# Rotary attention layer on one Trainium2 core: the depthwise convolution moved from the preparation to GpSimd in the attention loop, the values projected once and turned

## What is computed

```
q = xn @ wq.T + bq
k = (xn @ wk.T + bk) * scaling
v = xn @ wv.T + bv
lepe = conv_5x5(v, lepe_w, one filter per channel, padding 2) + lepe_b
qr, kr = theta_shift(q), theta_shift(k)        # x * cos + rotate_every_two(x) * sin, per head
attn = softmax(qr @ kr.T + mask)               # per image and head, 1024 x 1024
out = attn @ v + lepe
x = x + out @ wo.T + bo
```

## Time and profile before

| | us |
|---|---|
| median of three runs | 8046.31 |
| span of the profiled execution, first to last instruction | 8043.7 |
| what this span leaves to the median of the runs | 2.6 |
| layers 0 to 2, up to the rotary layer | 5577.0 |
| rotary preparation | 673.6 |
| rotary attention | 1793.1 |

### The profile page before, as it was taken

The page is one execution under the profiler, slowest core; times in us unless marked ns, Lnnn a source line. Parts: engine busy times, 40 slices in busy tenths (PEclk is TensorE's granted clock), DMA queues, the critical chain, the costliest instruction groups (busy, mean ns, idle before and its releaser), DMA issues. The chain is left out here.

```text
span 8043.7 us, 157230 instructions
## 1 busy us (share of the span) xinstructions
PE 7011.3 (87%) x56704; PEld 4290.7 (53%) x56704; DVE 4978.2 (62%) x7151; ACT 3803.5 (47%) x7049; POOL 2019.4 (25%) x2407
## 2 busy tenths in 40 slices
PE   3999999999877899469999999997776799999999
PEld 2555555555555556345555555553332466666665
DVE  4555555555555666445555555554888577777776
ACT  0444444444522555224444444443111577777777
POOL 3344344334220000043443443441111000000000
PEclk7999999999988989779999999998766899999999
DMA  7776776776459756477667667664222555455453
GB/s 160 154 140 122 139 136 117 138 140 122 88 178 216 133 110 122 103 163 141 124 129 142 126 124 140 133 123 96 77 72 72 138 124 136 121 130 130 120 135 88
DMA packets 500587, 1025.92 MB, mean 128 GB/s; under 512 B 80391, under 2 KB 276680, under 8 KB 460568
## 3 DMA queue, kind: packets, MB, share of 16 engines
q1 hardware_dynamic: 452694, 932.07, 53.5%
q0 software_dynamic: 47360, 86.53, 6.6%
HBM read 670.94 MB, written 358.93 MB: 128 GB/s over the span
## 5 line engine op out<-in xcount | busy, mean ns | idle before, releaser
L1512 DVE TENSOR_REDUCE a_nmp<-a_S 128x2 f32<-128x1024 f32 x1536 | 1878.8, 1224 | 1153.3 <-PE a_S L1357 1139.9
L1616 ACT ACTIVATE a_PROB<-a_T 128x512 f32<-128x512 f32 x3072 | 1667.7, 595 | 1750.0 <-PE a_T L1336 1742.5
L1215 POOL CAST a_RF<-a_RL 32x512 fp32r<-32x512 f32 x1536 | 1297.7, 845 | 1138.5 <-DVE a_RL L1540 1046.6
L2397 DVE CUSTOM_DVE_ANT_0 a_X<-a_S,a_mask 128x1024 f32<-128x1024 f32 x768 | 916.9, 1222 | 466.0 <-PE a_S L2293 462.3
L2440 ACT ACTIVATE a_PROB<-a_T 128x512 f32<-128x512 f32 x1536 | 836.3, 602 | 291.6 <-PE a_T L2307 291.6
L1332 PE MATMUL a_T<-a_QW,a_KW 64*128 64x512 f32 x3072 | 799.5, 513 | 181.1 <-ACT a_PROB L1616 108.2
L1332 PEld LDWEIGHTS a_T<-a_QW,a_KW 64*128 64x128 f32 x3072 | 309.5, 190 | 1161.0 <-issue 1157.9
L1370 PE MATMUL a_O<-a_PROB,a_V 128*32 128x512 f32 x6144 | 898.8, 660 | 2.5 <-ACT a_PROB L1616 2.5
L2307 PE MATMUL a_T<-a_ident,a_X 128*128 128x128 f32 x6144 | 827.4, 278 | 3.7
L2307 PEld LDWEIGHTS a_T<-a_ident,a_X 128*128 128x128 f32 x6144 | 671.2, 141 | 201.3 <-issue 183.1
L1357 PEld LDWEIGHTS a_S<-a_KV,a_QV 64*128 64x128 f32 x6144 | 650.2, 199 | 120.8
(11 more groups left out here) (178 smaller groups left out, 9248.2 us busy)
## 6 DMA issues: line engine op xcount, KB each, us to landing
a_QV<-a_part_rows SPq DMA_DIRECT2D x384, 256.0 KB, 7.7
a_rel_rows<-a_RF SPq DMA_DIRECT2D x96, 1024.0 KB, 9.2
a_K<-part_rows SPq DMA_DIRECT2D x576, 128.0 KB, 4.1
a_part_rows<-a_part SPq DMA_DIRECT2D x48, 1024.0 KB, 16.9
a_QV<-a_part_rows SPq DMA_DIRECT2D x384, 128.0 KB, 8.2
a_QV<-a_rel_rows SPq DMA_DIRECT2D x384, 128.0 KB, 7.9
a_QW<-a_rel_rows SPq DMA_DIRECT2D x192, 256.0 KB, 9.9
a_mask<-L_mask SPq DMA_DIRECT2D x48, 1024.0 KB, 8.6
```

The costliest lines, as they stand in the source:

```text
L1215: nc.gpsimd.tensor_copy(dst, src).then_inc(permuted, 1)
L1512: nc.vector.tensor_reduce(nmp[:, qh, c, 2 * pr:2 * pr + 2, kh], S[:, pr], AX.X, ALU.max).then_inc(s_done, 1)
L1616: nc.scalar.activation(PROB[:, s % PRING, 2 * pr + sd], T[:, slot(("st", s, pr, sd))], ACT.Exp).then_inc(t_act, 1)
L2397: nc.vector.tensor_tensor_reduce(out=X[:, v % 2, c, g], in0=S[:, sd].rearrange("p a b -> p (a b)"), in1=mask[:, n % 2, g, c], scale=1.0, s ...
```

## The change

- **Preparation.** Values are projected once, by channel, with the pair's two images in the two halves of the partitions (`by_channel`); PE transposes them for the values by token (`by_token`). ScalarE takes each tile twice, to `VC` and to the padded `VP`. SP stores the padded tiles to a new scratch tensor `pad_rows`. VectorE convolves only the first quarter of the first group (25 taps on 256 elements per pair) into `lepe_rows`. The projection of the convolution and its accumulating stores are gone. The copy of the stream to the output is issued image by image.
- **Attention.** GpSimd makes the other 44 convolutions, each for one pair of images, one group of heads and one quarter: 25 multiplications and 24 additions on 256 elements, two of them ahead of the loop and one before each even store. Each result goes to `lepe_rows`, comes back one head at a time into the rows of `LP`, and VectorE adds it to the divided output before `wo` (`add_lepe`). PE's `wo` waits for that addition. SP loads pads and convolution rows in the same list as the operands.
- **Around it.** All semaphores of the earlier layers are cleared and freed, with a barrier, ahead of the rotary layer. The output bias sits in a row of `wo`.

```diff
-    RING, BLOCKS = 6, 3
+    RING, BLOCKS, HELD = 7, 3, 4
+    TURNS = (("vc", 0, 0), ("vc", 0, 1), ("vc", 1, 0), ("vt", 0, 0), ("vc", 1, 1), ("vt", 0, 1),
+             ("vc", 2, 0), ("vt", 1, 0), ("vc", 2, 1), ("vt", 1, 1), ("vt", 2, 0), ("vt", 2, 1))
...
+                if odd:
+                    sp.wait_ge(t_act, TALLY[("vt", p, GROUPS - 1, 1)])
+                    alone(sp)
+                    for g in range(GROUPS):
+                        sp.dma_start(pad_rows[g, p], VP[:, p % 2, g].rearrange("p y x -> p (y x)")).then_inc(pad_stored, 16)
+                    for o in range(2):
+                        sp.dma_start(v_rows[2 * p + o], VT[:, o]).then_inc(v_stored, 16)
+                    sp.wait_ge(taps, N_TAPS * (p + 1))
+                    alone(sp)
+                    sp.dma_start(lepe_rows[0, p], CV[:, p % 2]).then_inc(cv_stored, 16)
...
+            def by_channel(p, g, t):
+                n = ("vc", p, g, t)
+                free(n)
+                alone(pe)
+                for k in range(2):
+                    for odd in range(2):
+                        last = nc.tensor.matmul(T[64 * odd:64 * odd + 64, slot(n)], wv[:, k, 64 * g:64 * g + 64],
+                                                XN[:, (2 * p + odd) % HELD, k, t * BANK:(t + 1) * BANK],
+                                                start=k == 0, stop=k == 1)
+                last.then_inc(t_ready, 1)
+
+            def by_token(p, g, t):
+                n = ("vt", p, g, t)
+                free(n)
+                pe.wait_ge(t_act, TALLY[("vc", p, g, t)])
+                alone(pe)
+                for c in range(4):
+                    last = nc.tensor.transpose(T[:, slot(n), P * c:P * c + P], VC[:, (2 * g + t) % 3, P * c:P * c + P],
+                                               ident_sb[:])
+                last.then_inc(t_ready, 1)
...
-            for j, k in TAPS_EVEN:
-                tap(IMAGES // 2 - 1, j, k)
...
+            def padded(j):
+                (hg, qq), p = divmod(j // PAIRS_N, 4), j % PAIRS_N
+                need(sp, accumulated, N_TAPS * (j - FIRST - PADS + 1))
...
+            def lepe(v):
...
+                if j >= FIRST:
+                    sp.wait_ge(conv_stored[j % 2], 16 * ((j - FIRST) // 2 + 1))
...
+            def tap(j, k):
...
+                else:
+                    need(pool, accumulated, N_TAPS * (j - FIRST) + k - 2)
+                    dst = tapped[:, k % 3].rearrange("p (y x) -> p y x", x=SIDE)
+                    nc.gpsimd.tensor_scalar(dst, src, lw[:, hg, k:k + 1], None, ALU.mult).then_inc(multiplied, 1)
+
+            def add_tap(j, k):
+                pool.wait_ge(multiplied, (N_TAPS - 1) * (j - FIRST) + k)
+                pool.wait_ge(accumulated, N_TAPS * (j - FIRST) + k)
+                alone(pool)
+                nc.gpsimd.tensor_tensor(CV[:, j % 2], CV[:, j % 2], tapped[:, k % 3], ALU.add).then_inc(accumulated, 1)
+
+            def convolve(j):
+                tap(j, 0)
+                tap(j, 1)
+                for k in range(2, N_TAPS):
+                    tap(j, k)
+                    add_tap(j, k - 1)
+                add_tap(j, N_TAPS - 1)
...
+            for j in range(FIRST, FIRST + EARLY):
+                convolve(j)
             for v in range(UNITS):
+                j = FIRST + EARLY + v // 2
+                if v % 2 == 0 and j < CONVS:
+                    convolve(j)
                 store(v)
...
-                    pe.wait_ge(t_dve, upto(u, "turn", "dve"))
+                    pe.wait_ge(lepe_added, u)
...
-                    if sd == 0 and between is not None:
-                        divide(between)
+                    if between is not None:
+                        (add_lepe if sd else divide)(between)
...
+            sems.pop_all()
+            nc.clear_and_free_semaphores(nc.allocated_since(before))
+            nc.all_engine_barrier()
```

More of the change, by code:

```diff
@@ L1797, in _ @@
             sp.dma_start(X[:, 1], x_in[1]).then_inc(x_loaded[1], 16)
-            sp.wait_ge(consts_loaded, CONSTS)
-            alone(sp)
             for b in range(IMAGES):
-                sp.dma_start(stream_out[b], x_in[b]).then_inc(consts_loaded, 16)
-            for b in range(IMAGES):
+                p, odd = divmod(b, 2)
                 if b + 2 < IMAGES:
@@ L1828, in root @@
                 nc.gpsimd.tensor_tensor(rstd[:], var[:], power[:], ALU.pow).then_inc(powered, 1)
[L1830 to L1835, removed]
             nc.gpsimd.memset(power[:], -0.5).then_inc(pool_set, 1)
[L1838 to L1839 removed]
+            pool.wait_ge(pool_set, 1)
             root(0)
@@ L1874, in mean @@
                                  start=True, stop=True).then_inc(averaged, 1)
[L1876 to L1883, removed]
-                    for k in range(2):
-                        last = nc.tensor.matmul(T[at:at + count, slot(n)], wv[:, k, first:first + count],
-                                                XN[:, odd, k, t * BANK:(t + 1) * BANK], start=k == 0, stop=k == 1)
-                last.then_inc(t_ready, 1)
             def rotated(what, b, g, h):
@@ L1891, in rotated @@
                 free(n)
+                if what == "qk" and g == 0 and h == 0:
+                    pe.wait_ge(xn_ready, 2 * b + 2)
                 alone(pe)
@@ L2069, in padded @@
-            def padded(p, j, t):
-                n = ("vc", p, j, t)
+                nc.scalar.copy(part[:, at, 0, h * BANK:(h + 1) * BANK], whole[:, n % BLOCKS]).then_inc(hi_done, 1)
+            def padded(p, g, t):
+                n = ("vc", p, g, t)
                 act.wait_ge(t_ready, AT[n] + 1)
-                if t == 0:
-                    need(act, taps, PAIR_TAPS * (p - 1))
+                if g == 0 and t == 0:
+                    need(act, pad_stored, 16 * GROUPS * (p - 1))
+                    need(act, taps, N_TAPS * (p - 1))
@@ L2099, in _ @@
+                for o in range(2):
+                    last = nc.scalar.copy(VT[:, o, 4 * t:4 * t + 4, G * g:G * g + G, 0:DIM], src[:, :, o])
+                last.then_inc(t_act, 1)
             for b in range(IMAGES):
-                p, odd = divmod(b, 2)
-                for j in ((1, 2) if odd else (0,)):
-                    for t in range(2):
-                        padded(p, j, t)
                 for i in range(PIECES):
-                    high(PIECES * b + i)
-                for j in range(4):
-                    values(b, j)
@@ L2108, in _ @@
-                if odd and p:
-                    outputs(b - 3)
-                    outputs(b - 2)
-            outputs(IMAGES - 2)
-            outputs(IMAGES - 1)
-def attend_rot(nc, sems, name, stream, w, ident, part_rows, v_rows):
+                    n = PIECES * b + i
+                    if n:
+                        high(n - 1)
+                    for what, p, g, t in turns(b, i):
+                        (padded if what == "vc" else values)(p, g, t)
+            high(PIECES * IMAGES - 1)
@@ L2231, in _ @@
             values(0)
-            for v in range(2, UNITS + 1):
+            for j in range(FIRST, FIRST + PADS):
+                padded(j)
+            for v in range(2, UNITS + 2):
                 if v < UNITS:
                     operands(v)
-                values(v - 1)
+                if v <= UNITS:
+                    values(v - 1)
+                lepe(v - 2)
                 n, b = divmod(v, IMAGES)
```

255 lines of the change are left out of this document (128 added, 127 removed).

## The result

The changed kernel takes **8195.54 us** (median, 8165.9 to 8205.51) where the kernel before takes 8047.07 us beside it (8032.21 to 8073.91): a ratio of 1.0171, 95% interval 1.0143 to 1.0199. It is 1.7% slower; 7714 us, 4.1% faster, was predicted, with a range that ended at 7960.

What follows compares the result with a forecast made beforehand. VectorE's convolution taps bound the preparation, PE the attention. 8043.7 - 376 + 5 + 13 (GpSimd's loop) + 20 + 1 (SP's loads) + 5 (VectorE's addition) = 7711.7, as a median 7714 us; range 7640 to 7960.

Steps and rivals of the forecast that it cites:

- Preparation: Rotary layer's preparation: 24 ahead, 245 for the images, 28 behind, so 297 us instead of 673, -376 us.
- the 10 us put aside for the burst: Preparation: padded tiles and value blocks go out in one burst; SP's later loads and part stores queue behind it, 10 us.
- rival 2: Preparation stays slow: PE waits for VectorE and keeps the half clock, 369 us instead of 297, about 7785; chance 0.15.
- The +5 for semaphores: Around the rotary layer: clearing semaphores and one more barrier, between 0 and 10.1 us, taken as +5.
- A multiplication lies between the copy, 0.35, and the addition, 0.68: Attention, GpSimd: a multiplication on 256 elements was taken as 0.46 us, nearer the copy.
- Addition 0.68: Attention, GpSimd: an addition on 256 elements, 0.73 us less 0.05 overlap with its neighbour, 0.68 us.
- Contention 5.4: Attention: VectorE's SBUF accesses hold GpSimd up by 5.4 us in two units.
- Issues and waits 3: Attention, GpSimd: three DMA issues at 0.96 us for each convolution, 3 us.
- The start: Attention: three convolutions of about 32 us precede the first store, issued at 118 us; PE waits +20 us, once.
- Rival 1: Attention: GpSimd becomes the bound of the loop, at 41 us a convolution about 7910 us; chance 0.27.
- 0.90 for faster: Whole kernel: chance 0.90 of faster, 0.02 of the same, 0.08 of slower.
- Rival 3, starvation: Attention: VectorE's subtraction gets in only when GpSimd's train ends, up to 1230 us, about 8930, slower than before; chance 0.08.

Runs made afterwards that it cites:

- Experiment 4: Changed kernel plus a last block in which GpSimd alone runs ten forms of multiplication, addition and copy, six of each; 8200.18 us with the block, one run.
- experiment 1: Changed kernel with a second operation, + 0.0, in the 24 GpSimd multiplications of each convolution; 8644.59 us, ratio 1.0728 to the kernel before.
- experiment 7: Changed kernel with the one-operation multiplication at every third tap, the two-operation form at the other 16, waits unchanged; 7818.1 us, one run.
- experiment 3: Changed kernel with VectorE's subtraction cut to 2 of 1024 elements and the exponent scaled by 0.001; 8216.45 us, one run.
- experiment 5: Changed kernel with two-operation GpSimd multiplications, each waiting for the addition right before it; 7754.08 us, one run.
- experiment 6: As experiment 5, and each GpSimd addition also waits for the multiplication right before it; 7952.15 us, one run.
- experiment 11: Experiment 8 with half a convolution ahead of each store and the break only before every second multiplication; 7685.96 us, ratio 0.9549 to the kernel before.
- experiment 8: Experiment 5 with no convolution ahead of the first store and SP's padded-row loads one pair later; 7737.81 us, ratio 0.9594 to the kernel before.

## Why the prediction was wrong, step by step

- **Preparation: right, and closer than its parts**, 296.4 against 297 us, in other executions 296.2 to 299.2. Ahead of the first image's matmuls lie 23.9 us for 24, the eight images take 249.9 for 245, and 22.6 follow them for 28: two errors that cancel. Among the images the even ones take 25 us each for 20.7 and the odd ones 36.2 to 38.5 for 38, so that the 10 us put aside for the burst came out elsewhere. VectorE had 219.8 us for 204 and PE 235.3 for 219 at full clock; the clock was 0.90, so rival 2 is out. The +5 for semaphores was never seen by itself.
- **The step that failed: "A multiplication lies between the copy, 0.35, and the addition, 0.68".** It measured 0.89. The bounds were taken from two operations that are not of its kind, on the thought that one input costs less than two. Experiment 4 shows that the form with one operation costs more than an addition of two tiles. 24 x (0.89 - 0.46) = 10.3 us a pair, and 46.9 - 36.6 = 10.3: the whole miss of the loop, as the smaller errors below cancel.
- **The other terms of the loop held.** Addition 0.68, measured 0.70. Contention 5.4: the mean distances from multiplication to addition (1.03 us, undisturbed 0.89), back (0.75, 0.70) and between the two last additions (1.74, 0.85) give 23 x 0.143 + 22 x 0.054 + 0.9 = 5.4. Issues and waits 3: from the last addition to the next convolution's start 3.2 less the addition's own 0.7, 2.5. With 24 x (0.89 + 0.70) + 0.53 + 0.15 = 38.8 of own work the sum is 46.7.
- **The start: mis-sized.** First store at 160 us for 118 predicted, because the three convolutions ahead of it take 44.2, 44.4 and 41.3 us instead of 32 each, and the first starts at 31 us instead of 22. That is 92 us more than in the kernel before, where 20 was predicted. From first to last store it is 401 us more (2120.2 against 1719.6 in the earlier trace rows): 41 turns of 46.9 us instead of 36.4 add 429, and the stores behind the last convolution give 28 back, since PE already had work done for them (the first pair comes 6.5 us after the one before it). With 3 for the tail this makes the 495.
- **Rival 1 was the right mechanism** (GpSimd sets the loop), at too low a price: 42.1 us was the upper end, and its 7910 went by 41. With 46.9 its own formula gives 7714 + 10.6 x 44 - 13 = 8167 us. So the sign of the result hung on one operation whose row the trace didn't have, and 0.90 for faster was far too sure.
- **Rival 3, starvation, was real**, only not in the changed kernel: it appears when the slow form goes and nothing else changes. That the changed kernel was spared was luck as far as the prediction goes, which knew neither the slow form nor that it lets VectorE in. It was priced at 28 us a pair, 1230 in all; experiment 1 measured 24.8 at the longest and 2754.6 - 1795.1 = 960 us for the stage. The counter-argument, a VectorE copy that got through between casts, was one row of other instructions and didn't hold here.
- The Trainium skill (GPSIMD Engine Reference, "Performance versus the Vector engine") gives 1.03 cycles an element for a loop body of up to two operations, and about 1.8 as the best case of a tight loop unrolled by four; the prediction took the two as the range of one-input work. The trace agrees for the two-operation form (0.8 ns an element is 1.0 cycle of 1.2 GHz) and neither figure fits the one-operation form (2.5 ns, 3.0 cycles); the measurement decides.
- The Trainium skill (SBUF — State Buffer, "Who interferes with whom") lets whoever issues first hold the shared pair until that instruction is finished. Taken instruction by instruction, VectorE would wait for one; in experiment 1 it waited through some forty that were issued after its own. The measurement decides.

**What stays open.** Why the long subtraction gets in at a one-operation multiplication (experiment 7), while one of two elements starves up to 20.1 us behind a train of the same form (experiment 3), no run shows. That a break lets the long one in soon is shown by experiments 5, 6 and 11. No run has breaks with the one-operation form at every tap, so what a break alone would do for the changed kernel is open too.

## What to carry to other kernels

Price each moved instruction by a row of its own form; if the trace has none, take a range beyond both neighbours and let it decide how sure the sign is. When GpSimd runs a long chain of short instructions beside a VectorE `tensor_scalar` in SBUF, give the chain a break (a wait for the instruction just issued) every two to four instructions: 0.13 us each, against tens of us of starvation. An engine whose turn is 3% longer than that of the engine that should set the loop (37.5 us against 36.4) is worth relieving of even a DMA issue: those 1.1 us decided whether the convolution was hidden. Work done in advance didn't replace it (experiment 8).

## What the runs showed of the hardware

- GpSimd's `tensor_scalar` with one operation: 0.90 us on 128x256, 1.54 on 128x512. With a second operation that adds zero: 0.45 on 128x256; with two columns 0.54 and 0.75. The additional operation halves the time (experiment 4).
- A GpSimd train without breaks shut a VectorE `tensor_scalar` of 128x1024 out for up to 24.8 us (own time 0.75); with a break of 0.13 to 0.2 us before every second, every or every fourth instruction (experiments 5, 6 and 11) the longest were 1.4, 2.0 and 2.6 us.
- VectorE's `tensor_tensor_reduce` (L2425, one input in PSUM) kept 1.22 us on average in all of these but experiment 3, where it stood behind a starved subtraction (up to 17.8 us).
